# Second pass of a gated attention block: logits and their maximum ahead of the heads, gated rows turned into another PSUM tensor

## The reference, cut to what matters

```
x = x + tanh(g_xattn) * xattn(ctx, layernorm(x))     # long convolution of ctx, gating, two feed-forward blocks
x = x + tanh(g_ffn)   * moe(layernorm(x))

xattn:  xr = ffn1(x);  y = xr * dcwhz;  y = ffn2(y)          # dcwhz: the convolved context
ffn:    silu(layernorm(x) @ W1 + b1) @ W2 + b2 + x
moe:    h = x @ Wm + bm                                       # 8 heads of 32 per row
        w = softmax(head @ expert_emb)                        # logits over 16 experts
        top 2 of w weigh gelu(head @ W1[e] + b1[e]) @ W2[e] + b2[e]
        out = combined @ Wo + bo
```

## Time and profile before

| | |
|---|---|
| three timed executions | 829.43 us median (823.39 to 832.95) |
| the profiled execution | 830.46 us, of which the span of the profile is 828.7 us |
| PE busy | 781.6 us, 94% of the span |
| ACT busy | 668.9 us, 81% |
| DVE busy | 531.6 us, 64% |
| POOL busy | 496.5 us, 60% |
| granted TensorE clock, mean | 0.984 |

### The profile page before, as it was taken

The page is one execution under the profiler, slowest core; times in us unless marked ns, Lnnn a source line. Parts: engine busy times, 40 slices in busy tenths (PEclk is TensorE's granted clock), DMA queues, the critical chain, the costliest instruction groups (busy, mean ns, idle before and its releaser), DMA issues.

```text
span 828.7 us, 23805 instructions
## 1 busy us (share of the span) xinstructions
PE 781.6 (94%) x9938; PEld 382.5 (46%) x9938; DVE 531.6 (64%) x984; ACT 668.9 (81%) x832; POOL 496.5 (60%) x390
## 2 busy tenths in 40 slices
PE   7999889889899998999899999999999999999997
PEld 2676556646566665333343433434334434434433
DVE  3899964547668783767466566665664664664444
ACT  4444753436867767879999999999999999999995
POOL 1265331018653433468578788787787787787675
PEclk9999999979999998999999999999999999999999
DMA  8990499951122322557455555555555545555542
GB/s 293 203 241 27 102 190 192 193 119 34 51 68 77 78 74 79 146 150 175 125 143 169 153 162 147 161 161 155 153 159 150 167 153 154 162 153 162 152 154 65
DMA packets 85027, 117.06 MB, mean 141 GB/s; under 512 B 13075, under 2 KB 65427, under 8 KB 84692
## 3 DMA queue, kind: packets, MB, share of 16 engines
q1 hardware_dynamic: 84920, 115.55, 52.8%
HBM read 101.28 MB, written 6.94 MB: 131 GB/s over the span
## 4 chain that ended last, share of the span: by engine, by line
PE 72%; DVE 8%; SPq 7%; ACT 6%; DMA 3%; issue 3%; POOL 2%; DVEq 0%; ACTq 0%
PE PB L754 25%; PE PA L742 17%; PE PT L742 8%; PE PB L566 5%; PE PA L549 5%; SPq L334 5%; PE PT L641 2%; PE PB L764 2%; DMA RA<-wpd 2%; PE PA L510 2%; DVE DC L994 1%; PE PT L526 1%; ACT WK L1344 1%; ACT WK L1341 1%; DVE WK L838 1%
## 5 line engine op out<-in xcount | busy, mean ns | idle before, releaser
L1571 POOL TENSOR_TENSOR WK<-WK 128x512 f32<-128x512 f32 x239 | 321.5, 1345 | 110.6 <-DVE WK L1257 100.5
L1477 ACT ACTIVATE WK<-PA 128x1024 f32<-128x1024 f32 x349 | 360.9, 1145 | 9.4 <-PE PA L742 8.9
L754 PE MATMUL PB<-WK,EW 128*32 128x512 f32 x2048 | 265.5, 594 | 0.4 <-DVE WK L1257 0.4
L742 PE MATMUL PA<-RA,EW 98*32 98x512 f16 x2792 | 201.2, 380 | 0.5 <-ACT WK L1477 0.5
L1477 ACT ACTIVATE WK<-PT 128x1024 f32<-128x1024 f32 x163 | 187.9, 1153 | 2.0 <-PE PT L742 1.6
L1504 POOL TENSOR_TENSOR WK<-WK 128x512 f16<-128x512 f32 x64 | 79.9, 1260 | 135.3 <-ACT WK L1344 133.6
L742 PEld LDWEIGHTS PA<-RA,EW 98*32 98x32 f16 x2792 | 67.2, 95 | 155.4 <-issue 74.6
L742 PE MATMUL PT<-RA,EW 98*32 98x512 f16 x1304 | 99.4, 381 | 4.8 <-ACT WK L1477 3.4
L754 PEld LDWEIGHTS PB<-WK,EW 128*32 128x32 f32 x2048 | 62.0, 111 | 53.3 <-DVE WK L1257 0.9
L1257 DVE SCALAR_TENSOR_TENSOR WK<-PB,CV,W2h 128x512 f32<-128x512 f32 x64 | 48.1, 751 | 49.3 <-PE PB L754 49.3
L1257 DVE SCALAR_TENSOR_TENSOR WK<-PB,CV,W2l 128x512 f32<-128x512 f32 x64 | 48.0, 750 | 46.1 <-PE PB L754 45.6
(11 more groups left out here) (208 smaller groups left out, 1088.3 us busy)
## 6 DMA issues: line engine op xcount, KB each, us to landing
RA<-wpd SPq DMA_DIRECT2D x128, 134.1 KB, 4.9
W1h<-wtd SPq DMA_DIRECT2D x128, 128.0 KB, 2.7
DC<-wtd SPq DMA_DIRECT2D x128, 128.0 KB, 2.8
W2h<-wtd SPq DMA_DIRECT2D x128, 128.0 KB, 2.7
W2l<-wtd SPq DMA_DIRECT2D x128, 128.0 KB, 2.8
WK<-in_x SPq DMA_DIRECT2D x15, 512.0 KB, 4.1
RA<-DC SPq DMA_DIRECT2D x96, 64.0 KB, 2.0
out<-WK SPq DMA_DIRECT2D x16, 256.0 KB, 2.8
```

The source lines that it names most:

```text
L742: m = pe.matmul(pre(k)[32 * j:32 * j + 32, 512 * q:512 * q + 512], EW1[0:98, 128 * e + 32 * j:128 * e + 32 * j + 32], TS[0:98, h, 512 * b: ...
L754: m = pe.matmul(o[32 * q:32 * q + 32, :], EW2[:, 32 * e:32 * e + 32], hb[:, 512 * q:512 * q + 512], start=True, stop=True)
L1477: ac.activation(HB[n % NH][:, 1024 * p:1024 * p + 1024], pre(k)[:, :], ACT.Gelu, scale=1.0 / (SC * SC)).then_inc(a_gelu, 1)
L1571: po_.tensor_tensor(AC[g], AC[g], PR[m % 3], ALU.add).then_inc(g_ac, 1)
```

## The change

Three things change, all in the second pass; nothing is added or left out of the computation.

1. PE does `logits(s-3)` before `heads(s-2)`.
2. DVE does `less_max(s-3)` before `heads_lo(s-2)`. In step 7, `norm_shift` of block 6 also goes in front of `heads_lo`.
3. `gated_turn` of blocks 3 to 7 writes banks 0 and 1 of PA, once ACT has read them (silu of the same step's `layer1`), and leaves the list of PT. The list keeps its parity, so every other use has the bank that it had. `third_turn` now follows the heads of the step before in the list, and waits for their `v_hl`.

```diff
@@ transposer_uses
         out += [("turn", turn3(s - 2), k) for k in range(2)]
         out += [("head", s - 2, g) for g in range(2)]
-        if s + 1 < NB:
-            out += [("turn", turn2(s + 1), k) for k in range(2)]
@@ pt
+        late_turns = [turn2(b) for b in range(3, NB)]
...
+            if kind == "turn" and i in late_turns:
+                return PA[:, 512 * k:512 * k + 512]
@@ tensor_program, turn
-                    if t >= NB:
+                    if t in late_turns:
+                        bank = pt("turn", t, k)
+                        pe.wait_ge(a_silu, 4 * (8 + late_turns.index(t) + 2) + k + 1)
+                    elif t >= NB:
                         bank = take_pt("turn", t, k)
@@ tensor_program, steps of the second pass
                 layer1(8 + s, turn2(s), W2)
-                if s >= 2:
-                    if s == 2:
-                        pe.wait_ge(v_wm, 1)
-                    heads(s - 2)
                 if s >= 3:
                     if s == 3:
                         pe.wait_ge(v_eb, 1)
                     pe.wait_ge(v_out, 8 + s)
                     logits(s - 3, PB[:, 0:512])
+                if s >= 2:
+                    if s == 2:
+                        pe.wait_ge(v_wm, 1)
+                    heads(s - 2)
                 if s + 1 < NB:
                     gated_turn(s + 1)
@@ vector_program, steps of the second pass
                 second_sum(s)
+                if s >= 3:
+                    less_max(s - 3, PB[:, 0:512])
+                if s == 7:
+                    norm_shift(norm3(6))
                 if s >= 2:
                     heads_lo(s - 2)
-                if s >= 1:
+                if 1 <= s < 7:
                     norm_shift(norm3(s - 1))
-                if s >= 3:
-                    less_max(s - 3, PB[:, 0:512])
```

## The result

The changed kernel took 817.01 us in the median of three executions (816.72 to 818.41), against 829.43 us before (823.39 to 832.95). The ratio is 0.9879, with a 95% interval of 0.9833 to 0.9924. Its profiled execution took 818.41 us with a span of 816.6 us. The forecast was 818.5 us, with a range of 812.5 to 825.5.

A forecast was written before the change was run, and what follows sets the result against it. PE was taken to bound the second pass, losing 8.2 us in two waits on DVE. Gains of 5.74 + 5.28 + 0.26 = 11.3 us, taken as 10.9, gave 829.43 - 10.9 = 818.5 us, range 812.5 to 825.5.

The forecast's parts named there:

- both waits: PE's second-pass waits on DVE: 4.0 us for `gated_turn`'s bank of PT, 4.2 us at `layer2` for `less_max` to free PB.
- The anchors: Predicted start times on PE in the changed profile: `layer2` of steps 4 to 7 and `third_turn(6)`, at 308.7.
- The three terms of the sum: Gains up to `layer2` of step 4 (5.74 us), over the three periods to step 7 (5.28), at the pass's end (0.26).
- The second count: Length minus PE's busy time over five stretches, 8.18 us; with the clock's 1.84 us a gain of 10.0 us.
- Step 2: Turn of block 3 on PE: 2.43 us of bank wait and 1.84 us of slow clock behind it vanish, 4.27 us.
- DVE as a check: Steps 3 to 6: DVE needs 15.2 to 15.7 us against PE's 16.05, so it fits by 0.4 to 0.8 us.
- rival A: DVE becomes the bound, with periods of about 16.9 us: gain 7.9 us, time 821.5; chance 0.25.
- The covers: Later low parts and the turns' silu wait stay hidden behind other work; uncovered, each costs at most 0.4 to 1.4 us a step.
- rival C: DVE and POOL collide at the port and `layer2` waits 1.1 us in five steps: gain 5.7 us, time 823.7; chance 0.10.
- rival D: `less_max` on DVE stalls on late transfers of the low parts; kernel slower, up to 838; chance 0.05 with any other loss.
- Rival B: Only the wait in step 2 goes, PE still waits 4.2 us at `layer2`: gain about 5 us, time 824.4; chance 0.10.
- The end of the pass: From the last of the steps' `layer2` to `third_turn(6)`: 17.96 us instead of 18.22, a gain of 0.26 us.

The follow-up runs named there:

- order_only: The kernel before with logits ahead of the heads on PE and the maximum ahead of the low parts on DVE, gated rows still through PT: ratio 0.9970.
- bank_only: The kernel before with only the gated rows of blocks 3 to 7 turned into PA, logits and maximum left behind the heads: ratio 0.9995.
- double_max: The changed kernel with one more, unused reduction of the logits (0.69 us) on DVE ahead of the maximum in steps 3 to 7: ratio 0.9868.
- late_shift: The changed kernel with `norm_shift` of block 6 in step 7 put back behind `heads_lo`: ratio 0.9900 to the kernel before.
- pe_early: The kernel before with the new banks and logits ahead of the heads on PE, but the maximum still behind the low parts on DVE: ratio 1.0057.

## Why the prediction was right

**The account of PE's waits was right; the closeness of the sum is partly luck.** The prediction took both waits away and counted what PE's own instructions leave. It got 16.05 us for a period, and the three later periods measured 48.14 / 3 = 16.05. But these are two misses that cancel. Where PE stopped for nothing, the period was 15.89 us (241.37 to 257.26). The count is 0.16 us too long, since it takes the first pair of `layer2` at its full 0.59 us, while the next matmul starts 0.43 us behind it (241.37 to 241.80). The wait of 0.32 us that was left in step 6 made that period 16.36 us and gave this back.

The anchors, moved by the 1.48 us that lie ahead of the stretch: `layer2` in step 4 at 242.6 against 242.85 measured, in step 5 at 258.7 against 258.74, in step 7 at 290.8 against 290.99, and `third_turn(6)` at 308.7 against 308.91. The three terms of the sum were 5.74, 5.28 and 0.26 us; measured are 5.52, 5.29 and 0.30, so 11.11 us in place of 11.3. The second count, from idle time (10.0), fell short by 1.1 us.

**Step 2** gave 4.43 us in this pair of profiles (10.81 us from the end of the heads to the next turn before, 6.38 after), where its term had 4.27. Two things about it were too simple. The clock's part is not there in every execution: order_only had the same idle time and kept its clock. And the 4.27 us are not certain by themselves, as "from below, only step 2 is nearly certain" claimed: bank_only gave most of them back at the next waits and by another fall of the clock, and gained nothing that the timed runs show. The lower bound should have been zero.

**DVE as a check** was a little too generous. It gave DVE 0.4 to 0.8 us to spare; in fact PE waited 0.38 and 0.32 us for the maximum in steps 3 and 6. In step 6 DVE itself was the bound: from the low parts at 273.05 to the end of the maximum at 289.37 it stops only for the 1.12 us of the round trip to POOL, and five routing instructions (279.85 to 282.45) stand in that time. double_max shows that the reading was still the right one for the steps together, and rival A, DVE as the bound of every period, is out.

**The covers** held as named: no wait for silus, none for low parts at `third_turn`, and POOL's low parts came in time. PE's waits for POOL are 0.9 us, as before, in steps that the change does not touch. So rival C did not occur as it was priced. But the collision itself moved, and fell on DVE as well, which the prediction had named as possible:

```profile
269.05 3.25 POOL L1511 TENSOR_TENSOR WK<-WK 128x512 f16<-128x512 f32 x2 [5.98 <-ACT WK L1351]
269.07 2.21 DVE L1048 SCALAR_TENSOR_TENSOR WK<-XR,SM,WK 128x1024 f32<-128x1024 f32 x1
```

POOL starts 0.02 us ahead, and `second_sum` takes 2.21 us instead of 1.27. It stayed hidden: DVE still waited 0.44 us for ACT's high parts two instructions later, and `layer2` at 273.15 began without a wait. DVE never waited for a transfer, so rival D did not occur. Rival B was wrong for the change, but its mechanism is what bank_only shows.

**The total** of 12.4 us by the medians exceeds the 10.9 forecast, but the timed runs cannot tell the two apart: the interval of the ratio, 0.9833 to 0.9924, is a gain of 6.3 to 13.9 us. In the profiles 11.11 us are the change's, of which 1.65 us are the fall of the clock that this profile of the kernel before had, and the rest is what the first pass and the part behind vary.

**The end of the pass** was worth 0.30 us. This is a gain of 1.0 us by the earlier shift, as late_shift shows, less the 0.70 us of logits that now run ahead of the last heads.

## What to carry to other kernels

When an engine waits twice in a loop for the same other engine, count the loop from its own instructions with both waits gone, and then expect less from either half alone: 4.3 us for the two halves apart, 9.5 together here, with the falls of the clock taken off. A reordering that spans two engines must be made on both; beside the new banks, DVE's order alone brought 4.0 us of 7.5, and PE's alone lost 2.1. Before two kernels are compared by one profile each, look where the clock fell in either: here one fall is 1.7 us, as much as some of the effects. And a saving at the start of a stage is only real if the next stall downstream is not where it is waited out or where moved work lands, as the exponentials showed.

## What the runs showed of the hardware that was not expected

- The TensorE clock after short idle time is not settled by the length of that time. Idle times of 2.43 us (before, step 2), 2.05 us (bank_only) and twice 2.18 us (pe_early) were followed by a slow clock; 2.43 us at the same place (order_only), 2.35 us (bank_only), 2.40 and once 2.18 us (pe_early) were not. Each of these falls cost 1.65 to 1.67 us. At the end of the pass 1.76 and 0.98 us of idle time were followed by a fall in both profiles of one program, and the `layer2` behind them took 6.72 us in one and 8.24 us in the other.
- POOL and DVE can slow each other by starting together. In step 5 of the changed kernel POOL started 0.02 us ahead of DVE, and DVE's instruction took 2.21 us instead of 1.27 and POOL's two 3.25 instead of 2.3. In step 3 of the kernel before, where DVE started 1.09 us behind POOL, POOL's two took 3.39 us and DVE's instruction still 1.27.
- The same program's profile repeats to 0.02 us over an 83 us stretch in which PE waits for no transfer. The end of the first pass, where PE waits for transfers and the clock is 0.84 to 1.00 (150 to 180 us), makes the heads of step 2 end anywhere from 219.3 to 225.7 us, over all profiles.
